# A layer norm folded into the stages on either side of it, in a fused perceiver block on one Trainium2 core

## The chip, the cores and the metric

The program runs on one core of one Trainium2 chip. The metric is the device time of one execution in microseconds (us). The median of three executions before the change is 3198.08 us. The profiled execution that every row below comes from took 3201.31 us, of which the span from the first to the last instruction is 3199.5 us.

## What is computed

A residual stream x of 16 x 64 tokens with 512 features (1024 tokens, 8 tiles of 128 tokens) goes through six layers. Only the first two matter here:

```python
# layer 1, context layer ("bidaf"): a similarity softmax over 1601 context rows, then
feats = concat([hc, hq_hat, hc * hq_hat, hc * hc_hat])      # 2048 features for each token
x = x + feats @ W_qv + b_qv
# layer 2, causal layer
n = layernorm(x)                                            # no gamma, no beta, eps 1e-5
q, k, v = (n @ Wq + bq) / sqrt(512), n @ Wk + bk, n @ Wv + bv
x = x + softmax(causal(q k^T)) v @ Wo + bo                  # 64 x 64 for each of 16 sequences
```

After them come a layer of experts, a cross attention over the same 1601 rows, a differential attention with its feed-forward, and a ternary feed-forward. Each of them is as long as before in the code, and the change leaves them alone.

Every float32 product is made of three TensorE products of float32r numbers: x is split into x_hi (a rounded copy, made by ScalarE) and x_lo = x - x_hi (made by VectorE), the weights likewise, and hi·hi + hi·lo + lo·hi is accumulated (`product`, L66).

## The kernel before, in words

The program is a chain of stages. Each is a block in which the five engines run their own instruction lists, held together by semaphores; the next stage's lists start when all engines have finished this one's. Nothing of a stage therefore lies beside another, apart from a transfer that a stage issues for a later one. In all the code, `wait_ge(semaphore, n)` holds the engine that executes it, and each engine executes in order.

**The context merge** (`bidaf_merge_stage`, L614) multiplies the 2048 features of a tile with W_qv. For tile t TensorE turns four feature parts of the next tile (`turn`, 4 transposes each, L816), computes the softmax mean (`mixing`, L804) and makes the four products of this tile (`merge`, 12 matmuls of 128x512 each, 48 for a tile). ScalarE and VectorE split the turned parts (`high`, `low`, L685). VectorE multiplies the context with the mean for the fourth part (`by_bar`, L706: TensorE's turn of the fourth part waits for it) and adds the result of a tile to x (`add`, L711). VectorE's order in pass t is written out by hand: by_bar(t+1), four lows, mixture and product for tile t+2, add(t). The results alternate between two banks, `out`. A last bank, `small`, is used at the start only. W_qv's first two parts come into `w_raw`, two buffers of 1 MB, which are dead once they are split.

**The norm stage of the causal layer** (`norm_stage`, L98, called at L1164 as "n1"): VectorE takes the statistics of 8 tiles, ScalarE loads the square-root table and takes one root, VectorE refines 1/sd in four small steps, normalises 8 tiles to `xn`, TensorE turns them (4 transposes for a tile), and ScalarE and VectorE split them to `a_hi` and `a_lo`.

**The projection** (`project_stage`, L900) runs a list of jobs; "pj0" makes qT, kT (FEATURES: weights stationary, 512 tokens moving) and v (TOKENWISE). A job has 8 units of 12 matmuls, with four banks for their results. In a FEATURES job, unit u is feature block u // 2 of token half u % 2, so the second unit already needs all tokens. The first job's weights come in four pieces, each loaded, split and used in turn; weights of later jobs go through the two raw buffers and are split while the job before runs. "pj1" is the same function with one RESIDUAL job: Wo is loaded and split at its start, GpSimd adds the bias to x, VectorE adds the products.

**The causal attention** (`causal_attention_stage`, L1055) lies between pj0 and pj1 and works tile by tile through a chain of small steps on four engines.

`TileNorm` (L211) is the norm cut up into calls that a stage can place where it likes (`gather`: statistics of one tile; `invert`: the chain up to 1/sd of a group of tiles, with ScalarE's `root` inside it; `apply`; `turn`; `high`; `low`). Two later layers use it before the change, always with a gamma.

Of the kernel before, what the change touches and what calls it, by code (L numbers as in the profile page):

```python
# [43 lines left out]
class Space:  # L44


    def __init__(self, nc, ctx, stage):
        self.nc, self.ctx, self.stage = nc, ctx, stage

    def sb(self, name, shape, dt=F32):  # L50
        return self.ctx.enter_context(self.nc.sbuf_tensor(f"{self.stage}_{name}", shape, dt))
# [4 lines left out]
    def sem(self, name):  # L56
        return self.ctx.enter_context(self.nc.semaphore(f"{self.stage}_{name}"))

# [152 lines left out]
class TileNorm:  # L211


    def __init__(self, nc, ctx, stage, x, ident, hi, lo, y, groups, gamma=None, beta=None, kept=None, affine=None, turned=None):
        s = Space(nc, ctx, stage)
# [11 lines left out]
            s.sem(n) for n in ("normed", "turned_ready", "hi_ready", "lo_ready"))  # L227
        self.links = self.mids = 0

# [11 lines left out]
    def invert(self, dve, g):  # L241
# [17 lines left out]
        self.link(dve, v.tensor_tensor(rstd, r0, r1, ALU.mult))  # L259

# [21 lines left out]
    def low(self, dve, t):  # L282
        dve.wait_ge(self.hi_ready, t + 1)
        ts = slice(t * P, (t + 1) * P)
        split_lo(self.nc, self.lo[:, :, ts], self.turned[:, t % 4, :].rearrange("p (k c) -> p k c", k=KC),
                 self.hi[:, :, ts]).then_inc(self.lo_ready, 1)
# [9 lines left out]
    def high(self, act, t):  # L296
        act.wait_ge(self.turned_ready, t + 1)
        split_hi(self.nc, self.hi[:, :, t * P:(t + 1) * P],
                 self.turned[:, t % 4, :].rearrange("p (k c) -> p k c", k=KC)).then_inc(self.hi_ready, 1)

    def turn(self, pe, t):
        pe.wait_ge(self.normed, t + 1)
        if t >= 4:
            pe.wait_ge(self.lo_ready, t - 3)
        for k in range(KC):
            last = pe.transpose(self.turned[:, t % 4, k * P:(k + 1) * P], self.y[:, t % self.ring, k * P:(k + 1) * P], self.ident[:])
        last.then_inc(self.turned_ready, 1)
# [306 lines left out]
def bidaf_merge_stage(nc, x_sb, hc, hq, neg_max, sc, ident, b_sim, W, bias, w_raw, w_loaded):  # L614
# [5 lines left out]
    with ExitStack() as ctx:  # L620
        s = Space(nc, ctx, "bm")
        w_hi, w_lo = s.sb("w_hi", [P, FC, D], F32R), s.sb("w_lo", [P, FC, D], F32R)
        w_more, more_loaded = s.sb("w_more", [P, 2, KC, D]), [s.sem("more_loaded0"), s.sem("more_loaded1")]
        f_hi, f_lo = s.sb("f_hi", [P, 2, FC, P], F32R), s.sb("f_lo", [P, 2, FC, P], F32R)
# [10 lines left out]
        small = s.ps("small", [P, 512])  # L635
# [18 lines left out]
        with nc.Block() as block:  # L654

            @block.sync
            def _(sp):
                sp.dma_start(bsim_sb[:], rows_of(b_sim, P)).then_inc(small_loaded, 16)
                sp.dma_start(bias_sb[:], rows_of(bias, P)).then_inc(small_loaded, 16)
                for c in (2, 3):  # L660
                    sp.dma_start(raw(c), W[c * D:(c + 1) * D, :].rearrange("(k p) n -> p k n", p=P)).then_inc(more_loaded[c - 2], 16)

# [12 lines left out]
            def _(dve):  # L675
# [82 lines left out]
                for t in range(2, TILES):  # L758
# [4 lines left out]
                    if t + 2 < TILES:  # L763
                        mixture(t + 2)
                        by_hq(t + 2)
                    add(t)

            @block.scalar
            def _(act):
# [24 lines left out]
                for t in range(2, TILES):  # L794
                    for c in range(4):
                        high(t, c)

            @block.tensor
            def _(pe):
# [56 lines left out]
                for t in range(2, TILES):  # L856
# [11 lines left out]
def bidaf_layer(nc, x_sb, ident, ctx_rows, ctx_cols, w_sim, b_sim, W, bias):  # L868
    with ExitStack() as ctx:
        s = Space(nc, ctx, "bidaf")  # L870
        hc = s.sb("hc", [P, TILES, D])
        hq = s.sb("hq", [P, TILES * D])
        neg_max, sc = s.sb("neg_max", [P, TILES]), s.sb("sc", [P, TILES])
        w_raw, w_loaded = s.sb("w_raw", [P, 2, KC, D]), [s.sem("w_loaded0"), s.sem("w_loaded1")]

        def load_first(sp):
# [2482 lines left out]
```

## Time and profile before

| | |
|---|---|
| median of 3 executions | 3198.08 us (3197.14 to 3198.80) |
| profiled execution | 3201.31 us, span 3199.5 us |
| TensorE matmul busy | 2904.0 us (91% of the span) |
| VectorE, ScalarE busy | 1641.0 us (51%), 1137.1 us (36%) |
| mean granted TensorE clock | 0.951 |
| last matmul of the merge, first of pj0 | 417.8 us, 438.8 us |
| last matmul of pj0, causal attention, first of pj1, end of pj1 | 507.1 us, 508.2 to 549.5 us, 554.0 us, 577.6 us |

In the rows, PE is TensorE (PEld its weight loads), DVE is VectorE, ACT is ScalarE, POOL is GpSimd and SP is SyncE, which issues the loads (SPq). L69 to L71 are the three products, L80 and L84 the two halves of a split: they are helpers, so the names of the tiles say which stage a row belongs to. A timeline row gives the start in us, the duration in us, what ran, how many were merged (x4), and in brackets how long the engine had been idle and what released it. PEclk is the clock granted to TensorE as a share of its full 2.4 GHz.

### The profile page before, as it was taken

Reading aid. Unit: us, or ns where it says so; the run is one execution under the profiler, and the core shown is the slowest. Engines: PE = TensorE matmul, PEld = TensorE weight load, DVE = VectorE, ACT = ScalarE, POOL = GpSimd, SP = SyncE. Lnnn points to the kernel's source line nnn. Section 1 sums busy time; section 2 is a strip of 40 time slices with the busy share of each in tenths; the row PEclk is TensorE's granted clock in tenths of the full one; section 3 lists DMA queues with packets and bytes.
Section 4 is the critical chain, followed back from the end, with each engine's and each line's share of the span. In section 5 each row is a group of like instructions: output and inputs, shape, how many; then the busy total and the mean of one; then the engine's idle time right before and its main releaser. Section 6 shows DMA issues by size and latency. Waiting matters only on the chain. (4 is left out here: it accounts for less than half of the span.)

```text
span 3199.5 us, 55477 instructions
## 1 busy us (share of the span) xinstructions
PE 2904.0 (91%) x23526; PEld 2287.4 (71%) x23532; DVE 1641.0 (51%) x3406; ACT 1137.1 (36%) x1803; POOL 83.8 (3%) x67
## 2 busy tenths in 40 slices
PE   6998987699998999999999999999999977789655
PEld 3444866588876888888888888888888866668522
DVE  4334433444444555555555555555555465764586
ACT  2112221222213433443433444334434332623384
POOL 0002000000000000000000000000000013010000
PEclk9999988899998999999999999999999988789877
DMA  7885010111113110111110111101111017511300
GB/s 271 310 293 205 1 43 17 40 47 52 39 34 122 37 40 21 38 45 45 32 35 24 45 45 37 40 20 40 45 45 35 28 57 152 68 34 46 118 1 27
DMA packets 170096, 213.84 MB, mean 67 GB/s; under 512 B 56064, under 2 KB 109312, under 8 KB 168976
## 3 DMA queue, kind: packets, MB, share of 16 engines
q1 hardware_dynamic: 148784, 206.40, 21.1%
q10 hardware_dynamic: 21088, 4.20, 0.9%
q8 instruction: 173, 2.83, 0.4%
q14 instruction: 51, 0.42, 0.0%
HBM read 197.97 MB, written 10.49 MB: 65 GB/s over the span
## 5 line engine op out<-in xcount | busy, mean ns | idle before, releaser
L69 PE MATMUL xa_J<-xa_c_hi,xa_wk_hi 128*128 128x402 f32 x1024 | 364.8, 356 | 5.9 <-DVE xa_c_lo L84 5.9
L1721 DVE CUSTOM_DVE_ANT_0 xa_pr<-xa_S,xa_m 128x402 f32<-128x402 f32 x512 | 271.1, 572 | 166.0 <-PE xa_S L1878 166.0
L71 PE MATMUL xa_J<-xa_c_hi,xa_wk_lo 128*128 128x402 f32 x1024 | 354.5, 346 | 0.0
L70 PE MATMUL xa_J<-xa_c_lo,xa_wk_hi 128*128 128x402 f32 x1024 | 354.5, 346 | 0.0
L69 PE MATMUL xa_J<-xa_wv_hi,xa_c_hi 128*128 128x512 f32 (+1 forms) x832 | 335.5, 403 | 0.0
L71 PE MATMUL xa_J<-xa_wv_hi,xa_c_lo 128*128 128x512 f32 (+1 forms) x832 | 327.3, 393 | 0.0
L70 PE MATMUL xa_J<-xa_wv_lo,xa_c_hi 128*128 128x512 f32 (+1 forms) x832 | 327.2, 393 | 0.0
L1606 ACT ACTIVATE xa_kT<-xa_J,cl_bk 128x402 f32<-128x402 f32 x256 | 152.1, 594 | 456.5 <-PE xa_J L71 453.3
L1748 DVE TENSOR_TENSOR cl_v<-xa_J,cl_bv 128x512 f32<-128x512 f32 (+1 forms) x208 | 143.6, 690 | 260.1 <-PE xa_J L71 222.4
L1622 ACT ACTIVATE xa_pr<-xa_pr,xa_nm 128x1608 f32<-128x1608 f32 x128 | 208.6, 1632 | 94.9 <-DVE xa_nm L1737 94.9
L69 PEld LDWEIGHTS xa_J<-xa_c_hi,xa_wk_hi 128*128 128x128 f32 x1024 | 193.0, 188 | 67.5 <-ACT xa_kT L1606 39.6
L84 DVE TENSOR_TENSOR xa_c_lo<-main_x,xa_c_hi 128x402 fp32r<-128x402 f32 (+1 forms) x256 | 131.5, 572 | 140.1 <-ACT xa_c_hi L80 140.1
L70 PEld LDWEIGHTS xa_J<-xa_c_lo,xa_wk_hi 128*128 128x128 f32 x1024 | 193.6, 189 | 0.7
L71 PEld LDWEIGHTS xa_J<-xa_c_hi,xa_wk_lo 128*128 128x128 f32 x1024 | 193.4, 189 | 0.0
L69 PEld LDWEIGHTS xa_J<-xa_wv_hi,xa_c_hi 128*128 128x128 f32 (+1 forms) x832 | 153.4, 184 | 54.7 <-ACT xa_kT L1606 10.1
L71 PEld LDWEIGHTS xa_J<-xa_wv_hi,xa_c_lo 128*128 128x128 f32 (+1 forms) x832 | 153.1, 184 | 40.1
L70 PEld LDWEIGHTS xa_J<-xa_wv_lo,xa_c_hi 128*128 128x128 f32 (+1 forms) x832 | 153.4, 184 | 34.9
L1631 ACT ACTIVATE xa_pT<-xa_T 128x512 f32<-128x512 f32 (+1 forms) x128 | 62.6, 489 | 232.2 <-PE xa_T L1897 228.5
L1756 DVE COPY xa_pT<-xa_S 128x512 f32<-128x512 f32 x128 | 86.9, 689 | 102.8 <-PE xa_S L1897 102.8
L1744 DVE TENSOR_SCALAR xa_pr<-xa_pr,xa_ri 128x1608 f32<-128x1608 f32 x128 | 135.3, 1057 | 4.5
L69 PE MATMUL ex_H<-moe_a_hi,ex_w_hi 128*128 128x512 f32 x320 | 127.6, 399 | 10.9 <-DVE ex_w_lo L84 10.9
L70 PE MATMUL ex_H<-moe_a_lo,ex_w_hi 128*128 128x512 f32 x320 | 127.3, 398 | 0.0
(439 smaller groups left out, 5381.5 us busy)
## 6 DMA issues: line engine op xcount, KB each, us to landing
bl_rows<-in_ctx SPq DMA_DIRECT2D x40, 1024.0 KB, 8.9
main_x<-in_ctx_cols SPq DMA_DIRECT2D x192, 201.0 KB, 2.6
bl_cols<-in_ctx_cols SPq DMA_DIRECT2D x24, 1024.0 KB, 10.5
main_x<-in_ctx_cols SPq DMA_DIRECT2D x64, 197.5 KB, 3.2
moe_raw<-in_L_ffn_routed_w SPq DMA_DIRECT2D x24, 512.0 KB, 3.9
main_qoT<-in_L_attn_W SPq DMA_DIRECT2D x16, 512.0 KB, 3.5
bl_early<-in_ctx SPq DMA_DIRECT2D x8, 768.0 KB, 12.4
ternx_raw<-in_L_ffn_w SPq DMA_DIRECT2D x4, 1024.0 KB, 8.0
```

Source lines behind the costliest of these rows:

```text
L69: pe.matmul(out, w_hi, x_hi, start=first, stop=False)
L70: pe.matmul(out, w_hi, x_lo, start=False, stop=False)
L71: return pe.matmul(out, w_lo, x_hi, start=False, stop=last)
L84: return nc.vector.tensor_tensor(lo, x, hi.bitcast(F32), ALU.subtract)
L1606: nc.scalar.activation(kT[:, s, j % 2, :], J[:, bank(b, ("k", u, j, s)), 0:KG], ACT.Identity, bias=bk_sb[:, 2 * u + s:2 * u + s + 1]).then ...
L1622: nc.scalar.activation(pr[:, r, :], pr[:, r, :], ACT.Exp, bias=nm[:, r:r + 1], accum_out=rs[:, r:r + 1]).then_inc(exp_done, 1)
L1631: nc.scalar.activation(pT[0:r, n0:n1, :], TURNED_IN[i][0:r, 0:(n1 - n0) * 2 * P].rearrange("p (n c) -> p n c", c=2 * P), ACT.Copy).then_in ...
L1721: nc.vector.tensor_tensor_reduce(out=pr[:, r, ks], in0=S[:, r, 0:KG], in1=m[:, ks], scale=1.0, scalar=NEVER, op0=ALU.add, op1=ALU.max, acc ...
L1744: nc.vector.tensor_scalar(pr[:, r, :], pr[:, r, :], ri[:, r:r + 1], None, ALU.mult).then_inc(scaled, 1)
L1748: nc.vector.tensor_tensor(v[0:rows(n), value_slot(b, n), :], J[0:rows(n), bank(b, ("v", n)), :], bv_sb[0:rows(n), :], ALU.add)\
L1756: nc.vector.tensor_copy(pT[:, n0:n1, :], TURNED_IN[i].rearrange("p (n c) -> p n c", c=2 * P)).then_inc(t_dve, 1)
```

## The change

The norm of the causal layer is no stage of its own any more; `bidaf_layer` and `causal_layer` become one function, `context_layers`, so that buffers can be shared.

- **In the merge**: VectorE takes the statistics of tile t right after add(t). After add(3) it inverts the first group (tiles 0 to 3). ScalarE loads the square-root table in pass 3, takes the root in pass 4 and normalises tiles 0 to 3 itself (`scale`, new), into the second half of `w_raw`. TensorE turns two of these tiles in pass 5 and two in pass 6, through the one bank `small`; ScalarE and VectorE split them. SyncE loads Wq into the first half of `w_raw` as soon as that half has been split, and waits for it at the stage's end.
- **In pj0**: Wq is there already. After the four split steps of Wq and the biases, VectorE inverts tiles 4 to 7, normalises and splits them. The units of the first job are in a new order (four feature blocks for the first 512 tokens, then four for the second). TensorE turns tiles 4 and 5 after unit 1, tiles 6 and 7 after unit 2, and waits for their low halves before unit 4. Wk goes into the buffer that holds the normalised tiles, so its load is issued only after tile 7 has been turned. Wo is loaded and split behind Wv, as a fourth set of weights.
- **In pj1**: no weights are loaded or split; the products start from the split Wo.
- a_hi and a_lo are kept as two halves of 512 tokens, allocated from the other end of the memory. Arguments `feeds` and `warm` of `project_stage` are new and unused here.

```diff
 class TileNorm:
+        self.shift, self.shift_ready = s.sb("shift", [P, TILES]), s.sem("shift_ready")
...
     def invert(self, dve, g):
         self.link(dve, v.tensor_tensor(rstd, r0, r1, ALU.mult))
+        if self.gamma is None:
+            v.scalar_tensor_tensor(self.shift[:, t0:t1], self.mv[:, t0:t1, 0], -1.0, self.rstd[:, 0, t0:t1], ALU.mult, ALU.mult)\
+                .then_inc(self.shift_ready, 1)
+
+    def scale(self, act, t):
+        for g, (t0, t1) in enumerate(self.groups):
+            if t0 <= t < t1:
+                act.wait_ge(self.shift_ready, g + 1)
+        if t >= self.ring:
+            act.wait_ge(self.turned_ready, t - self.ring + 1)
+        self.nc.scalar.activation(self.y[:, t % self.ring, :], self.x[:, t, :], ACT.Identity, bias=self.shift[:, t:t + 1],
+                                  scale=self.rstd[:, 0, t:t + 1]).then_inc(self.normed, 1)
...
 def bidaf_merge_stage(...):
+                sp.wait_ge(w_lo_ready, 1)
+                sp.dma_start(w_raw[:, 0], Wq.rearrange("(k p) n -> p k n", p=P)).then_inc(wq_loaded, 16)
+                sp.wait_ge(wq_loaded, 16)
...
                     nc.vector.tensor_tensor(x_sb[:, t, :], out[:, t % 2, :], x_sb[:, t, :], ALU.add).then_inc(added, 1)
+                    dve.wait_ge(added, t + 1)
+                    norm.gather(dve, t)
...
                     if t + 2 < TILES:
                         mixture(t + 2)
                         by_hq(t + 2)
+                    if t in (5, 6):
+                        norm.low(dve, 2 * t - 10)
+                        norm.low(dve, 2 * t - 9)
                     add(t)
+                    if t == 3:
+                        norm.invert(dve, 0)
...
                     for c in range(4):
                         high(t, c)
+                    if t == 3:
+                        norm.load_table(act)
+                    if t == 4:
+                        norm.root(act, 0)
+                        for n in range(4):
+                            norm.scale(act, n)
+                    if t >= 6:
+                        norm.high(act, 2 * t - 12)
+                        norm.high(act, 2 * t - 11)
...
                     merge(t, HC_PART)
+                    if t in (5, 6):
+                        norm.turn(pe, 2 * t - 10)
                     if t + 1 < TILES:
                         turn(t + 1, HB_PART)
-                    for c in range(1, 4):
-                        merge(t, c)
+                    merge(t, HQ_PART)
+                    merge(t, HH_PART)
+                    if t in (5, 6):
+                        norm.turn(pe, 2 * t - 9)
+                    merge(t, HB_PART)
...
 def project_stage(...):
+                for j in range(1, len(sources)):
                     if j >= 2:
+                        wait_after(sp, w_hi_ready, pieces + j - 2)
+                        wait_after(sp, w_lo_ready, pieces + j - 2)
+                    if j == 1 and norm is not None:
+                        sp.wait_ge(norm.turned_ready, TILES)
+                    sp.dma_start(raw[:, j % 2, :, :], sources[j].rearrange("(k p) n -> p k n", p=P)).then_inc(w_loaded[j % 2], 16)
...
+                    if norm is not None and j == 0:
+                        norm.root(act, 1)
+                        if n_bias:
+                            act.wait_ge(bias_ready, 1)
+                        keep(j, 0)
+                        keep(j, 1)
+                        norm.high(act, 4)
+                        norm.high(act, 5)
+                        keep(j, 2)
+                        norm.high(act, 6)
+                        norm.high(act, 7)
+                        keep(j, 3)
+                        if len(sources) > 1:
+                            take(1)
+                        for u in range(4, UNITS):
+                            keep(j, u)
+                        continue
...
+                if norm is not None:
+                    norm.invert(dve, 1)
+                    for t in range(4, TILES):
+                        norm.apply(dve, t)
+                    for t in range(4, TILES):
+                        norm.low(dve, t)
...
+                        if norm is not None and j == 0 and u == 4:
+                            pe.wait_ge(norm.lo_ready, TILES)
...
+                        if norm is not None and j == 0 and u in (1, 2):
+                            norm.turn(pe, 2 * u + 2)
+                            norm.turn(pe, 2 * u + 3)
...
-            norm_stage(nc, "n1", x_sb, xn, ident, hi=a_hi, lo=a_lo)
...
+            norm = TileNorm(nc, held, "n1", x_sb, ident, a_hi, a_lo, w_raw[:, 1], TOKEN_GROUPS, turned=(), side="right")
...
-        project_stage(nc, "pj1", a_hi, a_lo, [(RESIDUAL, Wo, bo, 1.0, x_sb)])
+        project_stage(nc, "pj1", a_hi, a_lo, [(RESIDUAL, Wo, bo, 1.0, x_sb)], first=(w_hi[:, 1], w_lo[:, 1]))
```

## Rows read from the trace of the kernel before

**Rows 1.** Busy time by stretch; columns are in the first line, times are us.
```profile
core 0: us, PE busy (x) PEld busy (x) DVE busy (x) ACT busy (x) POOL busy (x), PEclk, DMA share, GB/s
380.00:400.00 20.00, 20.00 (x103) 16.36 (x102) 8.38 (x14) 4.35 (x8) 0.00 (x0) 1.00 0.00 1
...
417.78:438.82 21.04, 6.09 (x32) 5.28 (x32) 16.54 (x41) 7.43 (x13) 0.00 (x0) 0.73 0.12 43
438.82:444.65 5.83, 5.83 (x14) 4.49 (x15) 2.00 (x3) 1.83 (x3) 0.00 (x0) 0.50 0.90 281
444.65:507.14 62.49, 62.48 (x276) 51.37 (x274) 9.67 (x11) 14.07 (x18) 0.00 (x0) 1.00 0.04 15
507.14:553.96 46.82, 26.77 (x137) 22.85 (x137) 16.60 (x51) 11.27 (x27) 0.65 (x3) 0.71 0.06 19
553.96:557.29 3.33, 3.33 (x8) 2.66 (x9) 2.01 (x3) 1.26 (x2) 1.00 (x1) 0.50 0.35 129
```

**Rows 2.** Timeline, end of the merge to the first matmul of pj0.
```profile
417.80 0.69 DVE L711 TENSOR_TENSOR main_x<-bm_out,main_x 128x512 f32<-128x512 f32 x1 [10.19 <-PE bm_out L71]
418.78 1.28 ACT L183 ACT_TABLE_LOAD   x1 [19.41 <-PEq L654]
...
437.41 1.29 ACT L80 ACTIVATE pj_w_hi<-pj_raw 128x512 fp32r<-128x512 f32 x2 [4.01 <-DMA pj_raw<-in_L_attn_Wq]
...
438.82 0.80 PE L69 MATMUL pj_out<-attn_a_hi,pj_w_hi 128*128 128x512 f32 x1 [6.05 <-DVE pj_w_lo L84]
```

**Rows 3.** Timeline, end of the causal attention, and the bias adds of pj1.
```profile
548.83 0.69 DVE L84 TENSOR_TENSOR attn_a_lo<-ca_C,attn_a_hi 128x512 fp32r<-128x512 f32 x1 [2.80 <-ACT attn_a_hi L80]
...
556.29 10.53 POOL L1022 TENSOR_TENSOR main_x<-main_x,pj_bias_row 128x512 f32<-128x512 f32 x8 [47.29 <-ACTq L930]
```

**Rows 4.** Timeline of TensorE in one merge pass, transposes only.
```profile
380.43 0.60 PE L816 MATMUL bm_turned<-main_ident,bidaf_hc 128*128 128x128 f32 x4
380.86 0.60 PE L816 MATMUL bm_turned<-main_ident,bidaf_hq 128*128 128x128 f32 x4
...
384.50 0.60 PE L816 MATMUL bm_turned<-main_ident,bm_hb 128*128 128x128 f32 x4
```

**Rows 5.** Timeline of VectorE in the same merge pass.
```profile
379.77 0.69 DVE L711 TENSOR_TENSOR main_x<-bm_out,main_x 128x512 f32<-128x512 f32 x1 [6.04 <-PE bm_out L71]
380.69 0.69 DVE L706 TENSOR_TENSOR bm_hb<-bidaf_hc,bm_bar 128x512 f32<-128x512 f32 x1 [0.24 <-PE bm_bar L804]
```

**Rows 6.** Timeline of VectorE, the same TileNorm calls in a later layer.
```profile
2600.74 0.69 DVE L2221 TENSOR_TENSOR main_x<-co_R,main_x 128x512 f32<-128x512 f32 x1 [0.29 <-PE co_R L71]
2601.47 0.69 DVE L239 BATCH_NORM_STATS2 con_stats<-main_x 128x6 f32<-128x512 f32 x1
...
2603.27 0.37 DVE L248 BATCH_NORM_AGGREGATE con_mv<-con_stats 128x2 f32<-128x6 f32 x4
...
2605.04 0.17 DVE L259 TENSOR_TENSOR con_rstd<-con_r 128x8 f32<-128x8 f32 x1
```

**Rows 7.** Timeline of ScalarE: the normalising pass of the first layer's norm.
```profile
16.97 0.81 ACT L191 ACTIVATE bidaf_hc<-main_x,n_shift,n_rstd 128x512 f32<-128x512 f32 x1 [1.28 <-DVE n_shift L165]
```

**Rows 8.** Transfers: count, size of each, median us from issue to landing.
```profile
bidaf_w_raw<-in_L_xattn_W_qv SPq DMA_DIRECT2D x2, 1024.0 KB, 15.1
...
pj_raw<-in_L_attn_Wk SPq DMA_DIRECT2D x1, 1024.0 KB, 6.5
...
n_gamma<-in_L_xattn_w_sim SPq DMA_DIRECT2D x1, 256.0 KB, 3.1
...
pj_bias_row<-in_L_attn_bv SPq DMA_DIRECT2D x1, 256.0 KB, 6.6
```

**Rows 9.** Timeline of ScalarE and VectorE: the two splits of a whole set of weights.
```profile
464.24 1.91 ACT L80 ACTIVATE pj_w_hi<-pj_raw 128x2048 fp32r<-128x2048 f32 x1
...
466.17 2.29 DVE L84 TENSOR_TENSOR pj_w_lo<-pj_raw,pj_w_hi 128x2048 fp32r<-128x2048 f32 x1 [17.85 <-ACT pj_w_hi L80]
```

**Rows 10.** Busy time by stretch: a shorter gap of TensorE between full stretches.
```profile
2784.31:2787.01 2.70, 0.00 (x0) 0.00 (x0) 2.67 (x6) 1.29 (x4) 0.00 (x0) 0.85 1.02 359
2787.01:2793.00 5.99, 5.99 (x14) 4.73 (x15) 1.74 (x6) 1.91 (x1) 0.00 (x0) 0.50 0.01 5
```

More of the change, by code:

```diff
@@ L634, in bidaf_merge_stage @@
         bar = s.ps("bar", [P, 512])
-        small = s.ps("small", [P, 512])
+        norm.turned = s.ps("small", [P, 1, 512])
+        small = norm.turned[:, 0, :]
         small_loaded = s.sem("small_loaded")
@@ L897, with project_stage @@
 FEATURES, TOKENWISE, RESIDUAL = range(3)
-def project_stage(nc, stage, a_hi, a_lo, jobs, prefetch=None, source=None, pieces=None):
+def project_stage(nc, stage, a_hi, a_lo, jobs, prefetch=None, weights=None, first=None, loaded=False, norm=None, feeds=None,
+                  ahead=None, warm=None):
     N = len(jobs)
     UNITS = 8
-    row_pieces = pieces or [[(0, k * P, P)] for k in range(KC)]
+    pieces = 0 if first is not None else KC
     with ExitStack() as ctx:
         s = Space(nc, ctx, stage)
-        raw = s.sb("raw", [P, 2, KC, D])
-        w_hi, w_lo = s.sb("w_hi", [P, 2, KC, D], F32R), s.sb("w_lo", [P, 2, KC, D], F32R)
+        if weights is not None:
+            raw, w_hi, w_lo = weights
+        elif N > 1 or first is None:
+            raw = s.sb("raw", [P, 2, KC, D])
+            w_hi, w_lo = s.sb("w_hi", [P, 2, KC, D], F32R), s.sb("w_lo", [P, 2, KC, D], F32R)
+        norm_turned = s.ps("turned", [P, 4, D]) if norm is not None or feeds is not None else None
@@ L923, in project_stage, with high_of, low_of, unit @@
         biased = [j[2] is not None for j in jobs]
+        sources = [W for _, W, _, _, _ in jobs] + ([ahead] if ahead is not None else [])
+        if norm is not None:
+            norm.turned = norm_turned
+        if feeds is not None:
+            feeds.turned = norm_turned
+        def high_of(j):
+            return first[0] if first is not None and j == 0 else w_hi[:, j % 2]
+        def low_of(j):
+            return first[1] if first is not None and j == 0 else w_lo[:, j % 2]
+        def unit(j, u):
+            return (u % KC, u // KC) if norm is not None and j == 0 else (u // HALVES, u % HALVES)
         def stored_before(j):
@@ L933, in _ @@
             def _(sp):
-                for k in range(KC):
-                    for p0, row, n in row_pieces[k]:
-                        sp.dma_start(raw[p0:p0 + n, 0, k, :], jobs[0][1][row:row + n, :]).then_inc(first_loaded[k], 16)
+                for k in range(0 if loaded else pieces):
+                    sp.dma_start(raw[:, 0, k, :], jobs[0][1][k * P:(k + 1) * P, :]).then_inc(first_loaded[k], 16)
                 for j, (kind, W, bias, scale, out) in enumerate(jobs):
@@ new lines, in _ @@
+                for k in range(pieces):
+                    if not loaded:
+                        act.wait_ge(first_loaded[k], 16)
+                    split_hi(nc, w_hi[:, 0, k, :], raw[:, 0, k, :]).then_inc(w_hi_ready, 1)
+                if warm is not None:
+                    warm.scalar(act)
+                if feeds is not None:
+                    feeds.load_table(act)
+                    feeds.root(act, 0)
+                    for t in range(4):
+                        feeds.scale(act, t)
+                    for t in range(4):
+                        feeds.high(act, t)
@@ new lines, in _ @@
+                for j in range(N):
+                    kind = jobs[j][0]
+                    if norm is not None and j == 0:
[15 more added lines that the diff above has]
+                        continue
+                    if j + 1 < len(sources):
```

188 lines of the change are left out of this document (99 added, 89 removed).

## The prediction, made before the changed kernel ran

> **What bounds the kernel now.** I read three views, in this order. First the busy time by stretch, with the borders put at the first and last matmul of each stage [rows 1]. In the merge TensorE is busy for all of its time at the full clock, 20.00 of 20.00 us, while VectorE has 8.38 and ScalarE 4.35 of the 20: TensorE sets the pace there, and what is given to the other two engines is free as long as TensorE never waits for it. The same holds in pj0 (62.48 of 62.49). Between the two lie 21.04 us in which TensorE does 6.09 us of transposes and no product; VectorE, with 16.54, is the busiest. That is the place to gain. The second view is the timeline of that hole [rows 2]: the merge's last add at 417.80, the next stage's first instruction at 418.78, the norm, then a wait for Wq's load, the first split at 437.41 and the first product at 438.82. The third is the same look at pj1's start: the causal attention ends with the split at 548.83 (until 549.52) [rows 3], the first product starts at 553.96 [rows 1], again after a load and a split. The rows show also what a hole costs afterwards: pj0's first 14 matmuls take 5.83 us at a granted clock of 0.50 (that is 1.2 of 2.4 GHz), against 62.48 / 276 = 0.2264 us each at 1.00, so 5.83 - 14 x 0.2264 = 2.7 us are lost; pj1's first 8 take 3.33, lost 1.5 [rows 1].
>
> **Part 1, the merge gets longer.** Four norm turns are added on TensorE. One costs the pitch of two such turns in a row, 380.86 - 380.43 = 0.43 us [rows 4]; 4 x 0.43 = **+1.7 us**, on the path. Everything else must hide:
> - Statistics behind each add: 0.73 from add to statistics and 0.69 for them [rows 6]. What is queued behind them on VectorE is by_bar, and TensorE's fourth turn waits for it. In the pass shown by_bar would end at 379.77 + 0.73 + 0.69 + 0.69 = 381.9 instead of 381.38 [rows 5]; TensorE comes to that turn at 384.50 [rows 4]. Hidden, with 2.6 us to spare.
> - In one pass the inversion lies there too. From the first aggregate to the end of rstd it takes 2605.21 - 2603.27 = 1.94 us, ScalarE's root inside it [rows 6], and the new shift step 0.2 more, by the small steps beside it (0.17 and a gap). by_bar then ends at 381.19 + 0.04 + 2.14 + 0.69 = 384.06 in that pass's time, against 384.50. Hidden, but by 0.4 us only. If it is not, one stall of some tenths; I take 0, and keep 0.5 for the range.
> - ScalarE: the table load is 1.28 [rows 2], four scalings 4 x 0.81 = 3.2 [rows 7], in different passes of 13.6 us of which ScalarE uses about a fifth (4.35 of 20) [rows 1]. The next tile's high halves are pushed back by these 3.2 us plus the wait for the inversion and are needed only a pass later. 0.
> - The one bank for the norm's turns makes each wait for the low half of the tile before. The two of a pass lie two part-products apart (24 x 0.2264 = 5.4 us), and one high and one low (0.6 to 0.8 each) fit in. 0.
> - Wq: one more transfer of 1 MB, behind the two that SyncE issues at the stage's start; more than 100 us remain until it is needed, so even the slowest such row, 15.1, hides it [rows 8]. 0.
>
> **Part 2, the hole.** The merge's last product ends 1.7 later, so the last add is at 419.5. Statistics of tile 7: to 419.5 + 0.73 + 0.69 = 420.95. From the end of the add to the next stage's first instruction it was 418.78 - 418.49 = 0.29 [rows 2], so the first split starts at 421.24. From first split to first product it was 438.82 - 437.41 = 1.41 [rows 2]: first product at **422.65** instead of 438.82, 16.17 us earlier, behind a gap of TensorE of 422.65 - 419.5 = 3.2 us instead of 21.
>
> **Part 3, pj0.** Before, 5.83 + 62.49 = 68.32 us from first to last product [rows 1]. Added: four turns, 4 x 0.43 = **+1.7**. The clock: the nearest row to the new gap of 3.2 us is one in which a gap of 2.70 us was followed by 14 matmuls in 5.99 us at 0.50 [rows 10], as after the long one, so I take the same loss of 2.7 and the part cancels. Ends: 0 lost (2.7 us more gain) and 0.4 more lost for the transposes. The new waits:
> - VectorE waits for three biases ahead of the inversion. Nothing is loading now, and the third is issued some 1.0 us into the stage, at 422.2. A 256 KB row took 3.1 alone and 6.6 behind 2 MB of weights [rows 8]: it lands at 425.3 to 428.8; two small scalings (0.17 each, as the small steps of [rows 6]), inversion and shift (2.14) and a first normalising pass (0.7 at most) give tile 4 at 428.5 to 432.0. TensorE asks for it after units 0 and 1: 422.65 + 5.83 + 10 x 0.2264 = 430.75. I take the lower end, as nothing lies ahead of it: no wait. The upper end gives 1.2 us.
> - The two column biases are copied as 512 single values each, and they stand ahead of the third in the same wait. The Trainium skill ("DMA: Bandwidth & Descriptors", § Rules for kernel authors) says that a non-contiguous last dimension lowers to one descriptor per element and advises against it. That speaks for the late end, and the gain would be 1.2 us less by it; the trace has them only behind a load of weights, so no row here shows which it is.
> - Tiles 6 and 7 must be split before unit 4. Their turns end at 430.75 + 0.87 + 2.72 + 0.87 = 435.2; unit 3 lasts until 437.9, and in those 2.7 us one eviction, two highs and a low (0.6 to 0.7 each, partly before) fit. 0.
> - Wk's load is issued at 435.2, when tile 7 is turned. It took 6.5 before [rows 8]: 441.7; splits 1.91 and 2.29 [rows 9]: 446.0. The second job starts at 435.2 + 5 x 2.72 = 448.8. Hidden, with 2.8 us to spare. ScalarE waits meanwhile with evictions of units 4 to 7 behind that wait; their banks are wanted from 448.8 on.
> - Wo's splits lie in the third job, 4.2 us ahead of VectorE's first add; the banks are wanted after 4 units, 10.9. 0.
>
> So pj0 ends 16.17 - 1.7 = **14.47 us** earlier than before.
>
> **Part 4, pj1.** The causal attention is the same code. pj1's first product needs nothing but the stage's start: 549.52 + 0.29 (as at the other border) = 549.81, against 553.96: **4.15 us** earlier. Its slow start stays (1.5 lost; up to 2.7 if it is as in pj0). GpSimd's bias adds are 10.53 / 8 = 1.32 each [rows 3] and start when the bias lands, 549.9 + 0.1 + 3.1 to 6.6; that is faster than the 2.72 of a unit, and the banks give four units of slack. 0.
>
> **Sum.** -14.47 - 4.15 = **-18.6 us**. The profiled execution would go from 3201.31 to 3182.7. It was 3.23 us above the median of the runs shown, so the median goes from 3198.08 to **3179.5 us** (-0.58%). 0.2%, or 6.4 us, is about what a measurement of this kernel can tell from no change.
>
> **Rivals.**
> (a) *The clock is kinder*: it stays up across the 3.2 us gap (2.7), pj1 starts fast (1.5), and the causal attention, whose mean with the hole is 0.71 and which so has slow and fast tiles by chance [rows 1], falls better (up to 3). Gain up to 26, typically 23: 3175. For: the gap is a seventh of the old one, and the clock fell only after some idle time in the old one too, whose mean is 0.73 [rows 1]. Against: in the nearest row it was down for all of the 5.99 us behind a still shorter gap [rows 10]. 0.13.
> (b) *A new wait in pj0*: Wk is late, because it is asked for 17 us after the stage's start instead of in its first microseconds, and Wv's load is issued right behind it on the same queue. If it lands after 15.1 as the pair of the merge did [rows 8], it is there at 450.3, split at 454.6, and TensorE stands 5.8 us: 3185.3; with the bias at its late end 3186.4. It begins to matter at a landing of 9.3. Against: those 15.1 were behind megabytes of context loads. 0.12.
> (c) *Slower*: pj0 loses its clock for good. Its units are now cut by turns that may wait for VectorE and evictions that wait for loads. With gaps of that kind the causal attention's stretch has a mean of 0.71 [rows 1]; if the 288 products of pj0 (65.3 us at full clock) ran so, they would take 65.3 x (1/0.71 - 1) = 26.7 more: 3206. It turns to a loss at 18.6 / 0.2 = 93 more slow matmuls. Against: the sum above finds no gap after the first product. 0.03.
> The Trainium skill ("TensorE: Matmul & The Clock Gate", § A second HAM failure mode: psum-queue depth-cycling) describes this case, short idle times between groups of matmuls that make the clock swing; that the attention swings agrees, and no row shows it for a projection.
> (d) *It doesn't do what it says*: half the norm merely moves, as TensorE waits in the merge for by_bar and in pj0 for the second half's chain, some microseconds each, up to 12 in all: gain under 6.4, 3192 and more. For: the 0.4 us margin. Against: all else has slack. 0.03.
> The forecast has the rest, **0.69**.
>
> **How the numbers follow.** The forecast's own bounds are +0.5 (by_bar), +1.2 (bias), +1.2 (pj1's clock), +0.4, and about 2 either way for the attention's clock: 3176 to 3184. The range takes in most of (a) and (b): 3174 to 3186.5. Faster by over 0.2%: 0.69 + 0.13 + 0.12 = 0.94; (d) and a part of (c) within 0.2%: 0.03; slower 0.03.
>
> **What would show it.** In the profile after: no norm stage; the last add of the merge about 1.7 us later; TensorE idle for about 3.2 us, then some 14 matmuls at 0.50; the turns of tiles 4 to 7 with no idle time of TensorE before them; the second job's first product without a wait for w_lo; pj1's first product 0.3 us behind the attention's last split. Wrong would be: TensorE idle before the merge's fourth turn, ahead of the turn of tile 4 or of the second job for more than a microsecond, or a granted clock under 1.00 after the first 7 us of pj0.

## The result and the profile after

The changed kernel takes 3181.73 us (median of 5, 3176.10 to 3184.51) against 3198.08 (median of 5, 3196.81 to 3200.49): ratio 0.9947, 95% interval 0.9933 to 0.9962. Forecast were 3179.5 and a range of 3174 to 3186.5. The profiled execution was the fastest of the five (3176.10 us, span 3174.3), 5.6 us under the median; so the stage times below say more than its total. Two timed executions, one of the kernel before in a later batch (5849.15 us) and one of `wo_only` (3922.16 us), took far longer than all others and are left out of every comparison. Busy time by stretch of the kernel after, borders at the first and last products as in [rows 1]:

```profile
core 0: us, PE busy (x) PEld busy (x) DVE busy (x) ACT busy (x) POOL busy (x), PEclk, DMA share, GB/s
380.00:400.00 20.00, 20.00 (x109) 16.65 (x108) 9.52 (x17) 5.56 (x11) 0.00 (x0) 1.00 0.00 1
418.75:421.92 3.17, 0.01 (x1) 0.01 (x1) 2.14 (x4) 1.41 (x3) 0.00 (x0) 1.00 0.05 0
421.92:427.54 5.62, 5.62 (x25) 4.43 (x25) 3.96 (x18) 1.56 (x4) 0.00 (x0) 1.00 0.24 47
427.54:432.10 4.56, 4.56 (x30) 3.97 (x29) 2.60 (x5) 2.32 (x5) 0.00 (x0) 1.00 0.00 0
432.10:489.46 57.36, 57.36 (x254) 47.13 (x252) 12.92 (x12) 15.28 (x19) 0.00 (x0) 1.00 0.17 55
489.46:530.78 41.32, 25.04 (x137) 21.24 (x137) 15.70 (x49) 10.02 (x25) 0.65 (x3) 0.78 0.00 1
530.78:536.31 5.53, 5.53 (x13) 4.36 (x14) 0.00 (x0) 0.00 (x0) 2.28 (x2) 0.50 0.17 50
536.31:555.40 19.09, 19.09 (x84) 15.45 (x83) 4.84 (x7) 0.00 (x0) 7.73 (x7) 1.00 0.00 0
```

In the merge (first row) TensorE is still busy for 20.00 of 20 us, with VectorE at 9.52 and ScalarE at 5.56 instead of 8.38 and 4.35: the norm's first half really lies beside it. TensorE's hole between merge and pj0 is 3.17 us instead of 21.04. What I had wrong is in the rows behind it: PEclk is 1.00 in the gap and in all of pj0, where I expected 0.50 for the first products; and pj1 starts at 0.50 for 5.53 us instead of 3.33.

The timeline of the kernel after at the same places as [rows 2, 5], first the pass with the inversion, then the border:

```profile
366.08 0.69 DVE L265 BATCH_NORM_STATS2 n_stats<-main_x 128x6 f32<-128x512 f32 x1
...
368.76 0.69 DVE L749 TENSOR_TENSOR bm_hb<-bidaf_hc,bm_bar 128x512 f32<-128x512 f32 x1
...
368.88 2.94 ACT L297 ACTIVATE bidaf_w_raw<-main_x,n_shift,n_rstd 128x512 f32<-128x512 f32 x4 [1.24 <-DVE n_shift L287]
...
370.08 0.60 PE L875 MATMUL bm_turned<-main_ident,bm_hb 128*128 128x128 f32 x4
...
418.79 0.69 DVE L754 TENSOR_TENSOR main_x<-bm_out,main_x 128x512 f32<-128x512 f32 x1 [9.46 <-PE bm_out L93]
419.51 0.69 DVE L265 BATCH_NORM_STATS2 n_stats<-main_x 128x6 f32<-128x512 f32 x1
...
420.51 2.19 ACT L102 ACTIVATE attn_w_hi<-bidaf_w_raw 128x512 fp32r<-128x512 f32 x4 [14.76 <-PEq L694]
...
421.92 0.50 PE L91 MATMUL pj_out<-attn_a_hi,attn_w_hi 128*128 128x512 f32 x1 [3.17 <-DVE attn_w_lo L106]
...
424.85 0.24 DVE L1118 TENSOR_SCALAR pj_bias_scaled<-pj_bias_col 128x4 f32<-128x4 f32 x2 [1.19 <-DMA pj_bias_row<-in_L_attn_bv]
...
426.94 1.91 DVE L307 TENSOR_SCALAR bidaf_w_raw<-main_x,n_mv,n_rstd 128x512 f32<-128x512 f32 x4
...
427.54 1.11 PE L344 MATMUL pj_turned<-main_ident,bidaf_w_raw 128*128 128x128 f32 x8
...
432.31 0.37 SPq L1049 DMA_DIRECT2D bidaf_w_raw<-in_L_attn_Wk  x1
...
438.19 1.92 ACT L102 ACTIVATE attn_w_hi<-bidaf_w_raw 128x2048 fp32r<-128x2048 f32 x1 [2.39 <-DMA bidaf_w_raw<-in_L_attn_Wk]
...
440.14 2.29 DVE L106 TENSOR_TENSOR attn_w_lo<-bidaf_w_raw,attn_w_hi 128x2048 fp32r<-128x2048 f32 x1 [6.20 <-ACT attn_w_hi L102]
...
530.78 0.76 PE L91 MATMUL pj_out<-attn_w_hi,attn_a_hi 128*128 128x512 f32 x1 [1.68 <-PEq L1218]
```

The fourth part's product ends at 368.76 + 0.69 = 369.45 and TensorE comes at 370.08: a margin of 0.63 us. The biases had landed 3.4 us after the third one's issue at 421.44 (424.85; VectorE waited 1.19); the two column biases, copied value by value, had taken only 2.1 and 2.3 us from their issues at 420.47 and 420.89. The first turn in pj0 starts right behind unit 1 with no idle time, Wk landed 5.9 us after its issue, and w_lo was ready at 442.4 for a second job that begins at 446.

The same stages in three profiles of the changed kernel (two of them from the experiments below), us. "Border and attention" is the time from pj0's last product to the attention's last:

| | before | forecast | after | again | again_2 |
|---|---|---|---|---|---|
| merge, first turn to last product | 119.5 | 121.2 | 120.9 | 121.2 | 121.1 |
| idle to first product | 21.05 | 3.2 | 3.17 | 3.17 | 3.16 |
| pj0, first to last product | 68.3 | 70.0 | 67.5 | 68.9 | 67.4 |
| border and attention | 41.0 | 41.0 | 39.6 | 41.0 | 39.3 |
| idle ahead of pj1 | 5.79 | 1.6 | 1.68 | 1.68 | 1.68 |
| pj1 | 23.6 | 23.6 | 24.6 | 24.0 | 24.8 |
| all that follows, unchanged code | 2621.9 | 2621.9 | 2618.9 | 2622.4 | 2619.1 |

### The profile page after: what moved, and what is told of

Same layout as the page of the kernel before. It is cut to its first block and busy times, and to the rows that moved or that the text cites. A ratio compares the mean times of both kernels' runs of the same rounds, so it can differ in the third digit from the quotient of the medians.

```text
span 3174.3 us, 55470 instructions
## 1 busy us (share of the span) xinstructions
PE 2897.3 (91%) x23526; PEld 2278.3 (72%) x23532; DVE 1639.7 (52%) x3407; ACT 1138.9 (36%) x1805; POOL 81.8 (3%) x67
## 5 line engine op out<-in xcount | busy, mean ns | idle before, releaser
L91 PEld LDWEIGHTS xa_J<-xa_c_hi,xa_wk_hi 128*128 128x128 f32 x1024 | 193.0, 188 | 67.5 <-ACT xa_kT L1736 39.6
```

Of the source, the lines that this page charges most:

```text
L91: pe.matmul(out, w_hi, x_hi, start=first, stop=False)
```

## The experiments

All edits are to the changed kernel unless it says otherwise; "..." marks lines left out. Each timed run compares with the kernel before on the same chip. Rows of busy time have the columns of the first fence above.

### again, again_2: the changed kernel once more

No edit.

> The changed kernel, unaltered, once more: a second profile, and the reference for the three runs beside it. Theory 1 (the step as predicted): the clock falls in TensorE's 3.2 us gap ahead of the first product of the causal layer, so the first 12 to 14 products run at 0.50 and the projection takes 70.0 us from first to last product. Theory 2 (rival a): the gap is too short for it, the clock stays at 1.00 and the projection takes 67.5 us as in the first profile. Either way the median should be within 0.2% of 3181.7 us.

Measured: 3181.42 us against 3200.0, ratio 0.9939 (0.9926 to 0.9953). Here the clock did fall, but only for 3.03 us of the products:

```profile
core 0: us, PE busy (x) PEld busy (x) DVE busy (x) ACT busy (x) POOL busy (x), PEclk, DMA share, GB/s
418.56:421.72 3.16, 0.00 (x0) 0.00 (x0) 2.13 (x4) 1.40 (x3) 0.00 (x0) 0.94 0.05 0
421.72:424.75 3.03, 3.03 (x7) 2.45 (x8) 1.80 (x4) 0.79 (x2) 0.00 (x0) 0.50 0.48 88
424.75:490.60 65.85, 65.85 (x298) 54.24 (x297) 17.68 (x31) 18.61 (x24) 0.00 (x0) 1.00 0.14 48
```

7 products at 0.50: 3.03 - 7 x 0.2264 = 1.4 us lost, and pj0 is 68.88 - 67.54 = 1.3 us longer than in the profile where the clock stayed up. Neither theory holds as stated: the clock falls sometimes, and costs half of what I took.

> The changed kernel, unaltered, on the same chip as the two beside it. Median 3180 to 3183 us. In the three profiles so far of kernels with a gap of 3.2 us (unaltered twice, once with Wo late) the clock stayed up once and fell for 3.4 us twice; if the fall is a matter of chance with a short stretch behind it, the projection takes 67.5 or about 69 us here, and never the 70.0 that I predicted.

Measured: 3177.42 us against 3199.87, ratio 0.9932 (0.9920 to 0.9944); the clock stayed at 1.00 through the gap and pj0 took 67.42. The median is 4 us under those of the other two batches and under the 3180 to 3183 that I expected. Over the six profiles in this study of kernels whose gap is 3.2 us, the clock stayed up in three (`after`, `again_2`, `wk_later`) and fell in three. In `again` it fell just before the first product; in `wo_late` (below) and `long_chain` it stayed up through the gap and fell only after 1.3 and 0.9 us of products, again for 3.4 us, and pj0 took 69.07 us in both:

```profile
422.53:423.84 1.31, 1.30 (x6) 1.08 (x7) 1.31 (x3) 0.79 (x2) 0.00 (x0) 1.00 0.43 54
423.84:427.25 3.41, 3.41 (x10) 2.63 (x9) 1.81 (x12) 0.41 (x2) 0.00 (x0) 0.50 0.15 57
427.25:491.61 64.36, 64.36 (x292) 53.05 (x290) 14.18 (x20) 16.29 (x22) 0.00 (x0) 1.00 0.10 33
```

### wq_late: without the early load of Wq

```diff
-                sp.wait_ge(w_lo_ready, 1)
-                sp.dma_start(w_raw[:, 0], Wq.rearrange("(k p) n -> p k n", p=P)).then_inc(wq_loaded, 16)
-                sp.wait_ge(wq_loaded, 16)
...
-                                                 (TOKENWISE, Wv, bv, 1.0, v)], weights=(w_raw, w_hi, w_lo), loaded=True, norm=norm, ahead=Wo)
+                                                 (TOKENWISE, Wv, bv, 1.0, v)], weights=(w_raw, w_hi, w_lo), norm=norm, ahead=Wo)
```

> Only the early load of Wq is undone: its four pieces are issued at the projection's start. Both theories: the first split waits for the first piece, 2.7 us after the stage's first issue as before the change (437.41 - 434.70), so the first product comes 2.7 to 3.2 us later and TensorE's gap grows to about 6 us. Theory 1: nothing else changes, 2.7 to 3.2 us slower than the changed kernel. Theory 2: the clock, which had stayed up, now falls as well, and the loss is 5.4 to 6 us.

Measured: 3182.16 us (3180.88 to 3184.86), ratio 0.9949 (0.9935 to 0.9962), 0.7 us over `again` beside it, where theory 1 had 2.7 to 3.2 and theory 2 5.4 to 6. The intervals of the two overlap, so the total alone decides nothing. The stages do:

```profile
419.25:425.21 5.96, 0.00 (x1) 0.00 (x1) 2.13 (x4) 1.26 (x2) 0.00 (x0) 0.68 0.48 163
425.21:428.26 3.05, 3.05 (x7) 2.48 (x8) 2.17 (x7) 1.26 (x2) 0.00 (x0) 0.50 0.49 113
428.26:494.06 65.80, 65.80 (x298) 54.23 (x297) 17.46 (x29) 18.56 (x24) 0.00 (x0) 1.00 0.14 48
```

The gap grows from 3.17 to 5.96, the 2.8 us foreseen, and pj0 takes 68.85 us, as in `again` (68.88): against that profile only the gap is longer, as theory 1 has it. Of the 17.9 us taken from the hole, 2.8 are the early Wq and 15.1 the norm itself.

### wo_late and wo_only: the early Wo by itself

In `wo_late` it is undone:

```diff
-                                                 (TOKENWISE, Wv, bv, 1.0, v)], weights=(w_raw, w_hi, w_lo), loaded=True, norm=norm, ahead=Wo)
+                                                 (TOKENWISE, Wv, bv, 1.0, v)], weights=(w_raw, w_hi, w_lo), loaded=True, norm=norm)
-        project_stage(nc, "pj1", a_hi, a_lo, [(RESIDUAL, Wo, bo, 1.0, x_sb)], first=(w_hi[:, 1], w_lo[:, 1]))
+        raw_o = r.sb("raw_o", [P, 2, KC, D])
+        project_stage(nc, "pj1", a_hi, a_lo, [(RESIDUAL, Wo, bo, 1.0, x_sb)], weights=(raw_o, w_hi, w_lo))
```

> Only the early load and split of Wo are undone: they go back to the start of the output projection. Expected by the prediction's part 4: 4.1 us slower than the changed kernel, TensorE's idle time ahead of the first product of that stage 5.8 us instead of 1.7. A rival: the slow clock at this stage's start lasts longer when the stage starts early (5.5 us in the profile after, 3.3 before), so undoing it costs only 3 us.

Measured: 3186.57 us, ratio 0.9962 (0.9948 to 0.9975), 5.2 us over `again`, with intervals that just overlap. The profiled execution was the fastest of the five, 6.1 us under their median, so it can't account for the 5.2. The stretches ahead of and in pj1:

```profile
530.52:536.31 5.79, 0.00 (x1) 0.00 (x1) 1.44 (x3) 1.86 (x3) 0.00 (x0) 0.50 0.50 153
536.31:560.05 23.74, 23.74 (x96) 19.18 (x96) 6.80 (x10) 1.26 (x2) 10.55 (x8) 0.92 0.05 19
```

5.79 of idle time instead of 1.68 (4.1), and 23.74 for pj1 instead of 24.0 to 24.8. So these two stages give 3.0 to 3.9 us, which speaks for the rival more than for the full 4.1: the load's wait had also let pj1 begin nearer to the return of the clock. It came back 3.6 us behind the first product here and 3.3 before the change, against 5.5, 4.1 and 6.0 in `after`, `again` and `again_2`.

`wo_only` is the kernel before with the early Wo alone (the function `project_stage` of the changed kernel, so the bias loads stand ahead of Wk's):

```diff
-                                                 (TOKENWISE, Wv, bv, 1.0, v)])
+                                                 (TOKENWISE, Wv, bv, 1.0, v)], weights=(raw, w_hi, w_lo), ahead=Wo)
...
-        project_stage(nc, "pj1", a_hi, a_lo, [(RESIDUAL, Wo, bo, 1.0, x_sb)])
+        project_stage(nc, "pj1", a_hi, a_lo, [(RESIDUAL, Wo, bo, 1.0, x_sb)], first=(w_hi[:, 1], w_lo[:, 1]))
```

> The kernel before, with only the early load and split of Wo (the norm stage and the late Wq stay). Prediction's part 4: 4.1 us faster than the kernel before, TensorE's idle time ahead of the output projection 1.7 us instead of 5.8. Rival: less than 3, because the stage then starts in the slow clock for longer (up to 2.7 us lost against 1.5).

Measured: 3195.41 us (median of 11) against 3199.59 (of 15), ratio 0.9989 (0.9979 to 0.9998), that is 3.5 us with an interval of 0.6 to 6.7:

```profile
544.18:545.86 1.68, 0.00 (x1) 0.03 (x1) 0.69 (x1) 0.60 (x1) 0.00 (x0) 0.50 0.00 0
545.86:549.10 3.24, 3.24 (x8) 2.56 (x9) 0.00 (x0) 0.00 (x0) 0.13 (x1) 0.50 0.23 81
549.10:569.39 20.29, 20.29 (x90) 16.46 (x88) 4.84 (x7) 0.00 (x0) 9.90 (x8) 1.00 0.00 1
```

Here pj1 lost as much as before the change (8 products at 0.50), so its slow start is not always longer when it starts early. By the stages the early Wo is worth 4.2 us alone and 3.0 to 3.9 with the rest; the totals, 3.5 and 5.2, agree with that within their intervals and are no sharper.

### long_chain: is the margin in the merge real?

```diff
                     if t == 3:
+                        for n in range(12):
+                            norm.link(dve, nc.vector.tensor_scalar(norm.r2[:, 0, 0:4], x_sb[:, 0, 0:4], EPS, None, ALU.add))
                         norm.invert(dve, 0)
```

> Twelve small chained steps, about 0.2 us each and 2.4 us together, are put ahead of the inversion in the merge; their results are used by nobody. In the profile after, the fourth part's product ended at 369.45 and TensorE came to its turn at 370.08, a margin of 0.63. If that margin is all there is, TensorE now stands 2.4 - 0.6 = 1.8 us ahead of that turn in pass 4 and nowhere else, and the merge is 1.8 us longer. If the work beside TensorE is free whatever its length (the cover is larger than read), nothing changes.

Measured, one execution (3183.87 us): the twelve steps took 2.40 us, and TensorE stands 1.64 us, at that turn and nowhere else in the merge's later passes. The merge took 122.6 us, 1.4 to 1.7 more than in the three profiles of the changed kernel. Timeline of TensorE in `long_chain`:

```profile
370.31 0.39 PE L93 MATMUL bm_out<-bm_w_hi,bm_f_lo 128*128 128x512 f32 x1
372.34 0.66 PE L877 MATMUL bm_turned<-main_ident,bm_hb 128*128 128x128 f32 x4 [1.64 <-DVE bm_hb L749]
```

The cover ends where the two timelines said, to within 0.2 us (1.64 against 1.8).

### wk_later: is the margin ahead of the second job real?

```diff
                     if j == 1 and norm is not None:
                         sp.wait_ge(norm.turned_ready, TILES)
+                        sp.wait_ge(produced, 5)
```

> Wk's load waits for the fifth unit besides (unit 4's end, about 437.85 in the profile after, instead of 432.31). It landed 5.9 us after its issue: 443.7; splits of 1.91 and 2.29: 447.95, and the second job could start at 445.95. Expected: TensorE stands 2.0 us ahead of the second job, where it did not stand before. If rival b's mechanism did not exist (weights wanted later than I think), no idle time there.

Measured, one execution (3182.22 us); the rows are ScalarE's split of Wk and TensorE's first product of the second job:

```profile
445.93 1.92 ACT L102 ACTIVATE attn_w_hi<-bidaf_w_raw 128x2048 fp32r<-128x2048 f32 x1 [7.48 <-DMA bidaf_w_raw<-in_L_attn_Wk]
...
450.23 0.50 PE L91 MATMUL pj_out<-attn_a_hi,attn_w_hi 128*128 128x512 f32 x1 [1.63 <-DVE attn_w_lo L106]
```

There are 1.63 us of idle time where there was none (expected 2.0). Rival b's mechanism is real, and the change stays clear of it by 446.0 - 442.4 = 3.6 us.

### warm, warm_stats, warm_all: fillers for TensorE

`warm` fills most of the gap at the border, so that little idle time is left to TensorE there (0.3 us by its timeline):

```diff
                     merge(t, HB_PART)
+                for n in range(14):
+                    pe.transpose(bar[:, 0:P], ident[:], ident[:])
...
             def _(pe):
+                if norm is not None:
+                    for n in range(11):
+                        pe.transpose(out_ps[:, 3, 0:P], norm.ident[:], norm.ident[:])
```

> TensorE fills its gap: 14 transposes of the identity behind the last product of the merge, 11 at the start of the projection, into banks that nobody reads; the gap shrinks to the stage border, and nothing waits for them. Theory 1 (the clock falls in most executions): the median is 2.5 to 3 us under that of the changed kernel, and the first product runs at 1.00. Theory 2 (it never falls): the same median within 0.5 us. If it falls in some executions only: between the two, and with a smaller spread of the runs.

Measured: 3174.65 us, ratio 0.9925 (0.9912 to 0.9939), 6.8 us under `again` beside it. That is more than either theory has. By stages the first product came 3.2 us behind the last as before, at the full clock, and pj0 took 67.7: at most 1.3 us come from there, and nothing against the profiles in which the clock had stayed up. From the merge's last product to pj1's end it took 134.5 us, against 136.7, 138.7 and 136.4 in the three profiles of the changed kernel; the rest of this is in the attention (37.4 from first to last of its products, against 38.3 to 40.0) and pj1, which the edit does not touch. The largest part lies further behind, in code that it does not touch either: all that follows pj1 took 2615.1 us in the profile of `warm`, against 2618.9, 2622.4 and 2619.1. Some 3 to 6 us of that are in one stretch, the heads of the differential attention (from the first instruction on its `df` tiles to the first on its `dn` tiles): 94.1 us, against 97.9, 100.0 and 98.1. It is so in both profiles of `warm_stats` too (93.2 and 95.1), which has the same fillers, and hardly in those of `warm_all` (96.4 and 98.6). Why is not shown; the gap at the border does not account for the gain.

`warm_stats` adds to it:

```diff
-                    norm.gather(dve, t)
+                    if t + 1 < TILES:
+                        norm.gather(dve, t)
...
+                if norm is not None:
+                    norm.gather(dve, TILES - 1)
                 if n_bias:
                     dve.wait_ge(bias_loaded, 16 * n_bias)
```

> The kernel with TensorE's gap filled, and besides the statistics of tile 7 moved from the end of the merge into the projection, where VectorE waits 1.2 us for the biases. The merge's end is then 0.7 us earlier and the first product too: 0.7 us faster than the filled kernel, whose median was 3174.65; no later wait, since tile 4's turn comes after unit 1.

Measured: 3174.14 us, ratio 0.9921 (0.9908 to 0.9933), against 3174.65 in the other batch: no gain that can be told from none. Timeline of `warm_stats` at the border:

```profile
420.70 1.69 PE L932 MATMUL bm_bar<-main_ident 128*128 128x128 f32 x14
...
420.90 0.69 DVE L754 TENSOR_TENSOR main_x<-bm_out,main_x 128x512 f32<-128x512 f32 x1 [9.47 <-PE bm_out L93]
...
422.67 2.20 ACT L102 ACTIVATE attn_w_hi<-bidaf_w_raw 128x512 fp32r<-128x512 f32 x4 [14.81 <-PEq L694]
```

The fillers had been sized for a stage whose end waited for the statistics. With those gone, the fillers themselves (until 422.39) are what the border waits for; the add had ended at 421.59. They took back the 0.7 us: the first product came 3.22 us behind the last, as in `warm` (3.21).

`warm_all` also fills TensorE's waits in the attention:

```diff
+        idle = s.ps("idle", [P, 512])
...
+                    for n in range(6):
+                        pe.transpose(idle[:, 0:P], ident[:], ident[:])
                     pe.wait_ge(scaled, t + 1)
...
+                    for n in range(2):
+                        pe.transpose(idle[:, 0:P], ident[:], ident[:])
                     pe.wait_ge(pT_ready, t + 1)
...
                     last.then_inc(summed, 1)
+                for n in range(12):
+                    pe.transpose(idle[:, 0:P], ident[:], ident[:])
```

> The same, and TensorE's waits in the causal attention are filled too: six transposes of the identity ahead of each wait for the probabilities, two ahead of each wait for their transpose, twelve behind the last tile, into a bank that nobody reads. If the slow tiles of the attention (5.5 us against 4.2) come from the granted clock alone, it goes from 38 to 40 us to about 34 and the output projection starts at 1.00 (1.7 to 2.8 us less): 6 to 8 us faster than the variant without. If the fillers cost more than they give (at 0.50 six of them take 1.3 us, more than the wait of 1.1), no gain or a loss.

The attention and pj1, first in `warm_stats`, then in `warm_all`:

```profile
492.74:530.36 37.62, 24.06 (x136) 20.31 (x136) 14.37 (x47) 9.38 (x24) 0.62 (x3) 0.81 0.00 1
532.04:556.32 24.28, 24.28 (x96) 19.54 (x96) 4.84 (x7) 0.00 (x0) 10.03 (x8) 0.90 0.04 11
```

```profile
492.12:525.95 33.83, 26.26 (x202) 22.47 (x203) 14.08 (x47) 9.38 (x24) 0.61 (x3) 1.00 0.00 1
527.66:549.67 22.01, 22.01 (x96) 17.88 (x96) 4.84 (x7) 0.00 (x0) 10.05 (x8) 1.00 0.03 13
```

The attention goes to 33.8 us and pj1 to 22.0, both at a clock of 1.00: the slow tiles were the clock's. The second profiles have 33.8 and 22.0 again, against 38.7 and 24.0. From pj0's end to pj1's end it is 58.60 instead of 64.63, 6.0 us less. But the total was 3172.49, ratio 0.9917 (0.9903 to 0.9930), only 1.7 us less, where 6 to 8 were expected. Both were run again, side by side:

> The kernel with all of TensorE's waits filled, once more, next to the one without fillers in the attention. By stages its profile was 6.0 us shorter from the end of pj0 to the end of pj1 (58.60 against 64.63), but the medians differed by 1.7 us only, with runs scattered over 8. If the stage sums hold, five more runs of each bring the pooled difference to 4 to 6 us; if the fillers cost something elsewhere, it stays under 2.

> The kernel with only the gap between merge and projection filled and the statistics of tile 7 moved: the partner of the run beside it. Pooled median 3174 to 3175 us, 6 to 8 us under the changed kernel.

Measured: 3172.95 (0.9914, 0.9900 to 0.9929) and 3173.97 (0.9924, 0.9910 to 0.9937), 1.0 us apart. Pooled, the medians are 3172.7 (10 runs) and 3174.1 (12 runs), with means 2.4 us apart: the 4 to 6 of the stage sums failed, and the medians, 1.4 us apart, fit the other case (under 2). `again_2` beside them took 3177.42, so the fillers at the border are worth 3.4 us in this batch and 6.8 in the first. In the second profile of `warm_all` the attention's saving was there again (pj1 ended at 550.1, against 556.3), and all that follows took 2621.4 us instead of 2615.5 in its partner. In the first pair it took 2616.2 and 2615.9. Six us are gained early and more than half of them is not found in the medians. The code behind pj1 is the same, and in profiles of one and the same kernel it takes 2618.9 to 2622.4 (the changed kernel) and 2616.2 to 2621.4 (`warm_all`); whether the fillers lengthen it or the few profiles happen to say so is open.

## Why the prediction was right, and where its terms were off

The forecast (a gain of 18.6 us, 3179.5) held: 16.4, 18.6 and 22.4 us in three batches, whose 16 runs of the changed kernel have a median of 3179.1. The mechanism held too; that the total comes so close is partly luck (see that point below).

- **What bounds it** and **Part 1**: right. The merge is 1.4 to 1.7 us longer for four turns (forecast 1.7), and nothing else of the norm shows on TensorE. The inversion's margin was 0.63 (forecast 0.4); `long_chain` shows, to within 0.2 us, that it is the whole margin.
- **Part 2**: right to a tenth: the gap is 3.17 (forecast 3.2), and `wq_late` shows that it would be 2.8 us longer without the early Wq. (The sum there is off by 0.03: 419.5 + 0.73 + 0.69 is 420.92.)
- **Part 3**: the mis-sized term is the clock, "I take the same loss of 2.7". The row that I took it from showed 14 products at 0.50 behind a gap of 2.70 us; here there are none or 7. It cost 0 in two profiles of the unaltered kernel and 1.4 in one. I priced it from a single row. The trace of the kernel before has three more gaps of that size: behind 2.28 and 3.71 us it was slow for 6.5 and 7.3 us, behind 3.80 us only for the 2.66 of the rows below this list. So anything between the half loss and the full one stood there. So pj0 was 0.9 shorter to 0.6 longer than before instead of 1.7 longer: on average 2.1 us better than forecast. The four turns cost 67.5 - (68.3 - 2.7) = 1.9 (forecast 1.7). The waits were priced rightly: bias 3.4 us after its issue (between the ends 3.1 and 6.6), Wk 5.9 (forecast 6.5), none of them felt. What I cited of the Trainium skill ("DMA: Bandwidth & Descriptors", § Rules for kernel authors) did not bite here: the two biases that are copied value by value landed in 2.1 and 2.3 us, ahead of the third, and the wait ended 3.4 us after the last issue, near the lower end.
- **Part 4**: the idle time went from 5.79 to 1.68 (4.1, as forecast), but "its slow start stays (1.5 lost)" was too small: pj1 took 0.4 to 1.2 us more than before, which is inside the bound of 1.2 that I gave. `wo_late` agrees with it; in `wo_only` it did not happen.
- **Luck**: these two errors have opposite signs (2.1 too pessimistic, on average 0.9 too optimistic). The stages that I priced are 19.4 to 20.3 us shorter in the three profiles, where I had 18.6. Beside them the attention varies with unchanged code (39.3 to 41.0 us), and so does what follows (2618.9 to 2622.4). A median within 2.2 us of the forecast in the first batch says no more than that.
- **Rivals**: (a) came true in two of three profiles as to the gap, and pj0 was 2.5 to 2.6 us under the forecast there, near the 2.7 of that rival; against the profile in which the clock fell it is 1.3 to 1.5. Its second part did not come (pj1 started slow in all of them), and of the up to 3 us in the attention 1.4 to 1.7 did, in the same two profiles. (b) exists and begins to matter where I said within a microsecond (`wk_later`); Wk was asked for 11.8 us after the stage's first issue, and the 17 in its text should have been 14 by the times of part 3. (c) did not come: no profile of the changed kernel or a variant has a clock under 1.00 in pj0 after its first 4.8 us, also in `wk_later`, which has a gap in its middle. The swinging clock behind short idle times that the Trainium skill describes ("TensorE: Matmul & The Clock Gate", § A second HAM failure mode: psum-queue depth-cycling) has its case in the attention, where filling the short waits brought the mean from 0.81 to 1.00. (d) did not come: TensorE waits at none of the new places in the merge and pj0.

The gap of 3.80 us in the kernel before, and the matmuls behind it:

```profile
3155.24:3159.04 3.80, 0.00 (x0) 0.13 (x2) 3.46 (x4) 1.44 (x2) 0.00 (x0) 0.90 0.01 2
3159.04:3161.70 2.66, 2.66 (x7) 1.00 (x7) 2.66 (x3) 1.73 (x2) 0.00 (x0) 0.51 0.00 0
```

## What to carry to other kernels

A stage in which TensorE idles can be hidden piece by piece in its neighbours; price each piece by who is queued behind it on its own engine, and read the margin as the distance between two rows, the end of the last cover and the start of the waiting instruction. Lengthening one piece on purpose shows whether that margin is all. Time taken out ahead of a stage that starts at the slow clock can be partly given back there (0.4 to 1.2 of 4.1 us here, nothing in `wo_only`), and a median that moves less than the stages do needs the stages' own times.

## What the runs showed of the hardware

- After a gap of 3.2 us behind a fully busy stretch, one and the same program ran its next products at 2.4 GHz in two profiles and the first seven at 1.2 GHz in one. In two of three variants with the same gap the clock stayed up through the gap and fell after 1.3 and 0.9 us of products; in the third it never fell there. Behind 5.96 us there were also only 7 slow products; behind the 6.05 us before the change, 14 [rows 1, 2]. The clock had fallen 3.8 us ahead of the first product in `wq_late` (0.68 over the gap) and 1.0 us ahead of it before the change.
- Idle fillers on TensorE raised the attention's clock from 0.81 to 1.00 and made it 3.8 us shorter (in the second pair from 0.77 to 1.00, 4.9 us), although each tile got eight more transposes. A version with them all is the fastest here by a little: 0.9917 and 0.9914 of the kernel before, against 0.9932 to 0.9947 for the change itself.
- Fillers at a stage's end are part of the stage: once nothing else ended it, they did (`warm_stats`, until 422.39 against 421.59).
